# One core, 48 network steps in float32 halves: new orders on VectorE and ScalarE, and all the sums of a step's inner units on VectorE

## The chip, the core and the metric

One core of one Trainium2 chip runs the program. The metric is the device time of one execution, in microseconds (us). Engines: TensorE (PE, with its weight loads, PEld), VectorE (DVE), ScalarE (ACT), GpSimd (POOL), and SyncE (SP), which here only issues DMAs.

## The reference

`x` is (2, 2048, 512) in float32. Per batch entry b, three two-layer networks of 512 to 2048 to 512 units run over all tokens: an expert chosen by `itok_B_0_2[b]` and two shared ones. Their outputs are weighted by a softmax gate that is computed from the first token, and added to x; then one 512x512 matrix per entry, with a bias, is added.

```
s0, s1 = relu(x @ swi[0]) @ swo[0], relu(x @ swi[1]) @ swo[1]
eo     = relu(x @ wi[e]) @ wo[e]
w      = softmax(relu(concat(eo, s0, s1)[:, token 0] @ g1) @ g2)
x      = x + eo*w[0] + s0*w[1] + s1*w[2]
out    = x + (x @ W[c] + bias[c])
```

## The kernel before

**Tiling.** The 4096 tokens are four supers of 1024. A super takes 12 steps: three networks by four slices of 512 inner units, 48 steps in all. Step N consists of two up halves (n = 2N and 2N+1, 256 inner units each) and one down part. Each is a 2x2 block product by Strassen's scheme in Winograd's form, 7 products instead of 8. Each float32 operand is split into a high part (fp32r, copied by ScalarE: XH, WU, WD, HH) and a low part (original minus high, on VectorE: XL, WU, WD, HL), and a product is high x high + high x low + low x high. So an up product is 6 matmuls of 128x512 and a down product 12, and a step is 14*6 + 7*12 = 168 matmuls. Some steps carry 24 more, for the category matrix (`category`).

**The order of a step.** Every engine's order is written out by hand in a loop over m = -1 to 47. In step m the down part is that of step d = m and the up halves are a = 2N and b = 2N+1 of step N = m+1. TensorE's order is seven slots of up, up, down: a.0 a.1 and product 6 of the down part of step m-1; a.2 a.3 down.0; a.4 a.5 down.1; a.6 b.0 down.2; b.1 b.2 down.3; b.3 b.4 down.4; b.5 b.6 down.5. On the other engines `second(i)` stands for what follows a down product: VectorE adds its result to ACC (`add_sum`, L993 and L996), and where weights are being prepared, ScalarE (`down_high`, L710) and VectorE (`down_low`, L965) make the operands of a later down product.

**What an up half needs.** `first_product` (ACT L720), `seventh_product` (L726) and `chain` (L732, which fills u; product 4 waits for it) copy partial results; `block_22` (DVE L1007) and `block_21` (DVE L1016) finish two of four blocks of inner units. Product 6 waits for block_22, product 1 of the next half for block_21; relus follow on ScalarE.

**The sums.** From the four blocks of inner units, `hidden_sum` (L588) makes four sums for each half of the tokens' columns, eight a step, of 128x512. Before the change the four of half 0 run on GpSimd and the four of half 1 on VectorE. `hidden_high` (ACT L772) and `hidden_low` (DVE L976) split each operand of the down part; down product i waits for hidden_low i.

**The down part.** Product 1 is put on top of a copy of product 0, which ScalarE makes (`first_down_product`, L787) and which needs the banks of the step before to be free, so it waits for `add_sum(N - 1, 6)`.

**Preparing weights.** In the 12 steps of super 0 and in four of super 2, weights are met for the first time ("prepared"). GpSimd makes their block sums (`up_sums`, L604 to L609, and `down_sums`, L618 to L623), ScalarE and VectorE split them (`up_low`, L958), and SP stores the operands, which other supers load again. The GpSimd queue also makes the token sums of the next super (`token_sum`, L569, 128x1024), in steps 10, 22 and 34, whose tokens `token_high` (L682) and `token_low` (L949) split; up products of steps 11, 23 and 35 wait for them. `mix_add` (L1074) and what follows it weight the results of the super before, in some steps.

Queues run in the order of the program on each engine; waits are on semaphores. In VectorE's queue a step began, before the change, like this (a prepared step, token work left out):

```
for which in (0, 1, 3, 2): hidden_sum(dve, d, 1, which)
hidden_low 3, 1, 2;  add_sum(d - 1, 6) and one down_low
hidden_low 6;  up_low(b, 0);  one down_low;  block_22(a);  hidden_low 4
```

and ended `add_sum(d, 3)`, block_22(b), hidden_low(N, 0), `add_sum(d, 4)` and two down_low, block_21(b), up_low(b + 1, 1), `add_sum(d, 5)` and one down_low.

Of the kernel before, what the change touches and what calls it, by code (L numbers as in the profile page):

```python
# [57 lines left out]
LO_ORDER = [0, 3, 1, 2, 6, 4, 5]  # L58

# [110 lines left out]
def build(nc, xT, expert_id, category_id, wi, wo, swi, swo, g1, g2, W, bias, out):  # L170
# [11 lines left out]
    with ctx:  # L182
# [413 lines left out]
        def _(pool):  # L596
# [14 lines left out]
            def down_sums(N):  # L611
                k = 4 * PREP[N]
                A11, A12, A21, A22 = (PDR[:, q, :, :] for q in range(4))
                pool.wait_ge(s_pd, 16 * (PREP[N] + 1))
                if PREP[N] > 0:
                    pool.wait_ge(s_wld, PRODUCTS * PREP[N])

                pool.tensor_tensor(PDS[:, 0, :, :], A21, A22, ALU.add).then_inc(s_Sd, 1)  # L618
                pool.wait_ge(s_Sd, k + 1)
                pool.tensor_tensor(PDS[:, 1, :, :], PDS[:, 0, :, :], A11, ALU.subtract).then_inc(s_Sd, 1)  # L620
                pool.tensor_tensor(PDS[:, 2, :, :], A11, A21, ALU.subtract).then_inc(s_Sd, 1)
                pool.wait_ge(s_Sd, k + 2)
                pool.tensor_tensor(PDS[:, 3, :, :], A12, PDS[:, 1, :, :], ALU.subtract).then_inc(s_Sd, 1)  # L623
# [14 lines left out]
            for m in range(-1, STEPS):  # L638
# [3 lines left out]
                if d >= 0:  # L642
                    hidden_sum(pool, d, 0, 3)
# [7 lines left out]
                if N < STEPS:  # L651
                    hidden_sum(pool, N, 0, 0)
                    hidden_sum(pool, N, 0, 1)
                if end:
                    token_sum(pool, super_of(m) + 1, 2)
                if prepared(N):
                    down_sums(N)
                if N < STEPS:
                    hidden_sum(pool, N, 0, 2)
                if end:  # L660
                    token_sum(pool, super_of(m) + 1, 3)
                if m in (STEPS_SUPER, 3 * STEPS_SUPER):
                    category_identity(m // (2 * STEPS_SUPER))
# [9 lines left out]
        def _(act):  # L673
# [149 lines left out]
            for m in range(-1, STEPS):  # L823
# [10 lines left out]
                def second(i):  # L834

                    step, which = place_of(m, i)
                    if step >= 0:
                        begin_sum(step, which)
                    for e in made_after(step, which):
                        down_high(e // PRODUCTS, e % PRODUCTS)  # L840
# [5 lines left out]
                if more:  # L846
                    seventh_product(a)
                if m == -1:
# [8 lines left out]
                second(0)  # L857
                if d >= 0:
                    hidden_high(d, 6)
                if more:  # L860
                    chain(a)
                if start:
                    token_high(s + 1, 6)
                if more:
                    relu_11(a)
                if d > 0 and super_of(d) % 2 == 1 and rel == 1:
                    scale_sums(d)
                if d >= 0:
                    first_down_product(d)
# [73 lines left out]
        def _(dve):  # L943
# [161 lines left out]
            for m in range(-1, STEPS - 1):  # L1105
# [9 lines left out]
                def second(i):  # L1115
# [4 lines left out]
                    for e in made_after(step, which):  # L1120
                        down_low(e // PRODUCTS, e % PRODUCTS)
# [3 lines left out]
                    if m >= 0 and s % 2 == 0 and rel in (8, 9) and 1 <= i <= KD:  # L1125
                        gate_partial(s // 2, rel - 8, i - 1)

# [13 lines left out]
                if d >= 0:  # L1141
                    for which in (0, 1, 3, 2):
                        hidden_sum(dve, d, 1, which)
# [3 lines left out]
                if d >= 0:  # L1147
                    hidden_low(d, 3)
                    hidden_low(d, 1)
                    hidden_low(d, 2)  # L1150
                if start:
                    token_low(s + 1, 5)
                second(0)
# [34 lines left out]
                second(4)  # L1188
                out_part(1, 0)
# [9 lines left out]
                if gating:  # L1199
                    gate_max(s // 2)  # L1200
                block_21(b)
# [3 lines left out]
                if prepared_half(b + 1):  # L1205
                    up_low(b + 1, 1)
# [8 lines left out]
            for which in (0, 1, 3, 2):  # L1215
                hidden_sum(dve, t0, 1, which)
            for i in (3, 1, 2):
                hidden_low(t0, i)
            add_sum(t0 - 1, 6)
            hidden_low(t0, 6)  # L1220
            add_sum(t0, 1)
# [200 lines left out]
```

## Time and profile before

| | |
|---|---|
| median of 3 runs | 2019.12 us (2017.62 to 2020.86) |
| the profiled execution | 2017.75 us; its span on the core 2016.0 us |
| mean granted TensorE clock | 0.990 of full speed |
| busy share | PE 97%, DVE 65%, ACT 49%, POOL 27% |
| HBM | 223 GB/s over the span |

The 1.75 us between the profiled execution's time and its span lie around the program. All times in rows are counted from the span's start.

### The profile page before, as it was taken

The page shows a single profiled execution, that of the slowest core. Times are in us where ns is not written, and L with a number is a line of the kernel's source. Part 1 is how long each engine was busy: PE and PEld are TensorE (multiplying, and loading weights), DVE is VectorE, ACT ScalarE, POOL GpSimd, SP SyncE. Part 2 cuts the span into 40 slices and gives each one's busy share as a digit, 9 for nine tenths or more (in the row PEclk, how much of TensorE's full clock was granted, in tenths as well). Part 3 has the DMA queues.
Part 4 walks back from the last instruction along what each step waited for, and adds up shares of the span by engine and source line. Part 5 has one row for each costly group of instructions (what it writes and reads, how often), then busy time and mean ns, then how long its engine had stood idle before and what let it go on. Part 6 is the DMA issues. An engine that isn't in the chain of part 4 may idle for free. (4 is left out here: it accounts for less than half of the span.)

```text
span 2016.0 us, 25216 instructions
## 1 busy us (share of the span) xinstructions
PE 1950.9 (97%) x8504; PEld 1598.1 (79%) x8504; DVE 1317.7 (65%) x1378; ACT 981.4 (49%) x1441; POOL 542.3 (27%) x415
## 2 busy tenths in 40 slices
PE   6999999998999999999999999999989999999998
PEld 5777777786888888888788888887868788888886
DVE  6788788888645566455745554578885665555455
ACT  5655566556553444344544444456555533344441
POOL 4435534554112111111311111243541111111112
PEclk8999999999999999999999999999999999999999
DMA  5666656765876676566686676577658776756652
GB/s 214 237 246 258 256 224 250 303 259 221 260 246 215 203 234 215 181 196 195 226 267 200 198 225 203 190 280 271 263 199 264 242 231 208 219 184 194 196 168 107
DMA packets 187026, 450.99 MB, mean 224 GB/s; under 512 B 16916, under 2 KB 57876, under 8 KB 180500
## 3 DMA queue, kind: packets, MB, share of 16 engines
q1 hardware_dynamic: 186900, 449.39, 65.9%
q8 instruction: 70, 1.15, 0.2%
q14 instruction: 56, 0.46, 0.1%
HBM read 308.81 MB, written 140.51 MB: 223 GB/s over the span
## 5 line engine op out<-in xcount | busy, mean ns | idle before, releaser
L1268 PE MATMUL ups<-XH,WU 128*128 128x512 f32 x2688 | 895.1, 394 | 46.3 <-issue 24.2
L1268 PE MATMUL rps<-HH,WD 128*128 128x512 f32 x2688 | 884.8, 390 | 14.6 <-ACT rps L787 13.7
L1268 PEld LDWEIGHTS ups<-XH,WU 128*128 128x128 f32 x2688 | 508.7, 189 | 168.8 <-issue 26.1
L1268 PEld LDWEIGHTS rps<-HH,WD 128*128 128x128 f32 x2688 | 505.8, 188 | 125.7 <-ACT rps L787 18.7
L1268 PE MATMUL ups<-XL,WU 128*128 128x512 f32 x1344 | 526.9, 392 | 0.0
L1268 PE MATMUL rps<-HL,WD 128*128 128x512 f32 x1344 | 524.0, 390 | 0.0
L588 POOL TENSOR_TENSOR HT<-hid 128x512 f32<-128x512 f32 x96 | 136.8, 1424 | 944.1 <-PE rps L1268 944.1
L996 DVE SCALAR_TENSOR_TENSOR ACC<-rps,gw,ACC 128x1024 f32<-128x1024 f32 x129 | 165.3, 1282 | 221.4 <-PE rps L1268 221.2
L1268 PEld LDWEIGHTS ups<-XL,WU 128*128 128x128 f32 x1344 | 254.4, 189 | 51.3
L1268 PEld LDWEIGHTS rps<-HL,WD 128*128 128x128 f32 x1344 | 252.9, 188 | 52.1
L976 DVE TENSOR_TENSOR HL<-HT,HH 128x1024 fp32r<-128x1024 f32 x240 | 285.3, 1222 | 5.9 <-ACT HH L772 5.9
L772 ACT ACTIVATE HH<-HT 128x1024 fp32r<-128x1024 f32 x240 | 252.7, 1054 | 68.2 <-DVE HT L588 67.1
L993 DVE TENSOR_TENSOR ACC<-rps,ACC 128x1024 f32<-128x1024 f32 x124 | 151.3, 1220 | 105.9 <-PE rps L1268 105.8
L748 ACT ACTIVATE HT<-HT 128x512 f32<-128x512 f32 x96 | 60.7, 632 | 290.8 <-DVE HT L1016 290.7
L1007 DVE TENSOR_TENSOR hid<-ups,w 128x512 f32<-128x512 f32 x96 | 66.1, 688 | 131.4 <-PE ups L1268 131.4
L976 DVE TENSOR_TENSOR HL<-hid,HH 128x1024 fp32r<-128x1024 f32 x96 | 129.2, 1346 | 0.0
L740 ACT ACTIVATE hid<-ups 128x512 f32<-128x512 f32 x96 | 57.3, 597 | 128.4 <-PE ups L1268 128.4
L772 ACT ACTIVATE HH<-hid 128x1024 fp32r<-128x1024 f32 x96 | 101.7, 1059 | 23.4 <-PE rps L1268 21.8
L726 ACT ACTIVATE w<-ups 128x512 f32<-128x512 f32 x96 | 56.5, 589 | 112.3 <-PE ups L1268 112.3
L588 POOL TENSOR_TENSOR HT<-HT 128x512 f32<-128x512 f32 x48 | 64.7, 1347 | 137.1 <-PE rps L1268 137.1
L604 POOL TENSOR_TENSOR PUS<-PUR 128x256 f32<-128x256 f32 x32 | 24.8, 775 | 276.3 <-DVE WU L958 267.8
L744 ACT ACTIVATE hid<-hid 128x512 f32<-128x512 f32 x96 | 60.8, 633 | 72.9 <-DVE hid L1007 72.9
(105 smaller groups left out, 1607.9 us busy)
## 6 DMA issues: line engine op xcount, KB each, us to landing
WU<-wu_kept SPq DMA_DIRECT2D x448, 256.0 KB, 3.3
WD<-wd_kept SPq DMA_DIRECT2D x224, 512.0 KB, 3.3
wd_kept<-WD SPq DMA_DIRECT2D x112, 512.0 KB, 3.4
wu_kept<-WU SPq DMA_DIRECT2D x32, 1024.0 KB, 4.9
wu_kept<-WU SPq DMA_DIRECT2D x32, 768.0 KB, 3.7
sums_kept<-ACC SPq DMA_DIRECT2D x28, 512.0 KB, 5.2
MB<-sums_kept SPq DMA_DIRECT2D x28, 512.0 KB, 5.5
PUR<-in_L_cond_swi_dram SPq DMA_DIRECT2D x16, 512.0 KB, 6.1
```

What stands on the lines that cost most here:

```text
L588: eng.tensor_tensor(dst, p, q, op).then_inc(s_T[half], 1)
L604: pool.tensor_tensor(PUS[:, 2, :], A21, A22, ALU.add).then_inc(s_Su, 1)
L726: act.activation(w[:, :], ups[2][:, :], ACT.Copy).then_inc(s_w, 1)
L740: act.activation(hid[:, 0, half, :], ups[0][:, :], ACT.Relu).then_inc(s_relu, 1)
L744: act.activation(hid[:, 2, n % 2, :], hid[:, 2, n % 2, :], ACT.Relu).then_inc(s_relu, 1)
L748: act.activation(HT[:, 1, n % 2, :], HT[:, 1, n % 2, :], ACT.Relu).then_inc(s_relu, 1)
L772: act.activation(HH[:, i, :, :], src, ACT.Copy).then_inc(s_hhi, 1)
L976: dve.tensor_tensor(HL[:, i, :, :], src, HH[:, i, :, :].bitcast(F32), ALU.subtract).then_inc(s_hlo, 1)
L993: dve.tensor_tensor(ACC[:, j, :, :], src[:, :, :], ACC[:, j, :, :], ALU.add).then_inc(s_acc, 1)
L996: dve.scalar_tensor_tensor(out=ACC[:, j, :, :], in0=src[:, :, :], scalar=gw[:, g:g + 1], in1=ACC[:, j, :, :], op0=ALU.mult, op1=ALU.add).t ...
L1007: dve.tensor_tensor(hid[:, 2, half, :], ups[1][:, :], w[:, :], ALU.add).then_inc(s_ev, 1)
L1268: ins = pe.matmul(dst, stationary[a], moving[c], start=start and j == 0, stop=stop and j == 2, skip_group_check=True)
```

## The change

LO_ORDER, the order in which the low parts come, becomes 0, 1, 2, 3, 6, 4, 5. All eight sums of a step run on VectorE. On VectorE the step begins with three sums of half 1 and the last one of half 0, then the late `up_low`, and the `add_sum` of the step before stands behind one hidden_low instead of three; the down_low of the last slot is put off into the next step. The low parts of the next super's tokens (2 and 3) come ahead of the sums. On ScalarE `chain` is put ahead of hidden_high 6 and `first_down_product` ahead of `scale_sums`. GpSimd's `down_sums` is cut in two, with the last token sum between. The end of the program (from t0) gets the same order.

```diff
-LO_ORDER = [0, 3, 1, 2, 6, 4, 5]
+LO_ORDER = [0, 1, 2, 3, 6, 4, 5]
...
-            def down_sums(N):
+            def down_sums(N, late):
...
+                if late:
+                    pool.tensor_tensor(PDS[:, 2, :, :], A11, A21, ALU.subtract).then_inc(s_Sd, 1)
+                    pool.wait_ge(s_Sd, k + 2)
+                    pool.tensor_tensor(PDS[:, 3, :, :], A12, PDS[:, 1, :, :], ALU.subtract).then_inc(s_Sd, 1)
+                    return
...
@@ gpsimd, the loop @@
-                if d >= 0:
-                    hidden_sum(pool, d, 0, 3)
...
-                if N < STEPS:
-                    hidden_sum(pool, N, 0, 0)
-                    hidden_sum(pool, N, 0, 1)
                 if end:
                     token_sum(pool, super_of(m) + 1, 2)
                 if prepared(N):
-                    down_sums(N)
-                if N < STEPS:
-                    hidden_sum(pool, N, 0, 2)
+                    down_sums(N, False)
                 if end:
                     token_sum(pool, super_of(m) + 1, 3)
+                if prepared(N):
+                    down_sums(N, True)
@@ scalar @@
-                    for e in made_after(step, which):
+                    if i < PRODUCTS - 1:
+                        made(m, i)
+
+                def made(m, i):
+                    for e in made_after(*place_of(m, i)):
                         down_high(e // PRODUCTS, e % PRODUCTS)
...
                     seventh_product(a)
+                made(m - 1, PRODUCTS - 1)
...
                 second(0)
+                if more:
+                    chain(a)
                 if d >= 0:
                     hidden_high(d, 6)
-                if more:
-                    chain(a)
...
+                if d >= 0:
+                    first_down_product(d)
                 if d > 0 and super_of(d) % 2 == 1 and rel == 1:
                     scale_sums(d)
-                if d >= 0:
-                    first_down_product(d)
@@ vector @@
-                    for e in made_after(step, which):
-                        down_low(e // PRODUCTS, e % PRODUCTS)
+                    if 0 < i < PRODUCTS - 1:
+                        made(m, i)
...
-                if d >= 0:
-                    for which in (0, 1, 3, 2):
-                        hidden_sum(dve, d, 1, which)
                 if start:
                     token_low(s + 1, 2)
                     token_low(s + 1, 3)
                 if d >= 0:
-                    hidden_low(d, 3)
+                    hidden_sum(dve, d, 1, 0)
+                    hidden_sum(dve, d, 1, 1)
+                    hidden_sum(dve, d, 1, 3)
+                    hidden_sum(dve, d, 0, 3)
+                if m >= 0 and prepared_half(a):
+                    up_low(a, 1)
+                made(m - 1, PRODUCTS - 1)
+                if d >= 0:
                     hidden_low(d, 1)
-                    hidden_low(d, 2)
+                second(0)
                 if start:
                     token_low(s + 1, 5)
-                second(0)
+                if d >= 0:
+                    hidden_sum(dve, d, 1, 2)
+                    hidden_low(d, 2)
+                    hidden_low(d, 3)
+                made(m, 0)
...
                 second(4)
+                hidden_sum(dve, N, 0, 0)
+                hidden_sum(dve, N, 0, 1)
                 out_part(1, 0)
...
                     gate_max(s // 2)
+                hidden_sum(dve, N, 0, 2)
                 block_21(b)
...
-                if prepared_half(b + 1):
-                    up_low(b + 1, 1)
                 second(6)
@@ vector, the end @@
-            for which in (0, 1, 3, 2):
+            for which in (0, 1, 3):
                 hidden_sum(dve, t0, 1, which)
-            for i in (3, 1, 2):
-                hidden_low(t0, i)
+            hidden_sum(dve, t0, 0, 3)
             add_sum(t0 - 1, 6)
+            hidden_low(t0, 1)
+            hidden_sum(dve, t0, 1, 2)
+            hidden_low(t0, 2)
+            hidden_low(t0, 3)
+            add_sum(t0, 1)
             hidden_low(t0, 6)
-            add_sum(t0, 1)
```

## Rows read from the trace of the kernel before

**Rows 1.** The page: busy time of each engine, its share, instructions.

```profile
PE 1950.9 (97%) x8504; PEld 1598.1 (79%) x8504; DVE 1317.7 (65%) x1378; ACT 981.4 (49%) x1441; POOL 542.3 (27%) x415
```

**Rows 2.** Windows along step starts: stretch, its length, busy time (instructions), clock, DMA share, GB/s.

```profile
827.81:865.89 38.08, 38.08 (x170) 31.53 (x169) 20.82 (x21) 16.41 (x23) 5.21 (x4) 1.00 0.66 207
85.49:365.12 279.63, 270.77 (x1177) 219.42 (x1176) 227.24 (x248) 167.29 (x272) 132.60 (x113) 1.00 0.67 251
365.12:485.45 120.33, 116.31 (x505) 93.98 (x504) 100.86 (x112) 75.64 (x120) 57.39 (x44) 1.00 0.72 268
485.45:535.00 49.55, 40.85 (x169) 32.99 (x168) 35.81 (x33) 24.45 (x35) 16.05 (x10) 0.90 0.57 186
980.13:1020.42 40.29, 38.36 (x170) 31.45 (x168) 27.48 (x26) 20.02 (x28) 8.25 (x5) 1.00 0.61 196
1346.82:1466.77 119.95, 116.33 (x505) 93.97 (x504) 101.25 (x112) 74.98 (x119) 58.20 (x44) 1.00 0.71 267
1466.77:1515.53 48.76, 40.05 (x170) 32.43 (x169) 35.81 (x33) 24.26 (x35) 16.05 (x10) 0.93 0.58 191
```

**Rows 3.** Waits of TensorE in the whole span: us in total, times, longest.

```profile
PE ups L1268 <- issue: 24.2, 4, 8.1
PE rps L1268 <- ACT rps L787: 13.7, 12, 4.5
PE ups L1268 <- ACT u L732: 8.7, 11, 1.5
```

**Rows 4.** Timeline of VectorE in prepared step 3 (165.33 to 205.23): start, us.

```profile
167.68 0.69 DVE L958 TENSOR_TENSOR WU<-PUR,WU 128x512 fp32r<-128x512 f32 x1 [2.65 <-ACT WU L691]
...
171.03 1.22 DVE L588 TENSOR_TENSOR HT<-hid 128x512 f32<-128x512 f32 x1
...
174.72 3.49 DVE L976 TENSOR_TENSOR HL<-HT,HH 128x1024 fp32r<-128x1024 f32 x3
178.12 1.22 DVE L993 TENSOR_TENSOR ACC<-rps,ACC 128x1024 f32<-128x1024 f32 x1
...
182.61 0.68 DVE L1007 TENSOR_TENSOR hid<-ups,w 128x512 f32<-128x512 f32 x1
```

**Rows 5.** Timeline of TensorE in the same step.

```profile
180.58 0.50 PE L1268 MATMUL rps<-HH,WD 128*128 128x512 f32 x1 [0.69 <-ACT rps L787]
```

**Rows 6.** Timeline of GpSimd in the same step.

```profile
169.12 0.74 POOL L604 TENSOR_TENSOR PUS<-PUR 128x256 f32<-128x256 f32 x1 [2.24 <-DVE WU L958]
```

**Rows 7.** Groups of VectorE in the plain step of rows 2: busy, mean ns.

```profile
L588 DVE TENSOR_TENSOR HT<-hid 128x512 f32<-128x512 f32 x2 | 1.4, 688 | 0.0
```

**Rows 8.** The page's costliest groups, of the sums on GpSimd.

```profile
L588 POOL TENSOR_TENSOR HT<-hid 128x512 f32<-128x512 f32 x96 | 136.8, 1424 | 944.1 <-PE rps L1268 944.1
```

**Rows 9.** Timelines around the change of super, steps 10 and 11: VectorE, GpSimd, TensorE.

```profile
475.44 2.41 POOL L569 TENSOR_TENSOR XT<-XT,XS 128x1024 f32<-128x1024 f32 x1 [0.17 <-POOL XT L569]
...
480.11 0.68 DVE L1007 TENSOR_TENSOR hid<-ups,w 128x512 f32<-128x512 f32 x1
...
493.90 2.65 DVE L588 TENSOR_TENSOR HT<-HT,hid 128x512 f32<-128x512 f32 x1
...
493.21 2.79 POOL L569 TENSOR_TENSOR XT<-XT 128x1024 f32<-128x1024 f32 x1
...
500.06 0.76 PE L1268 MATMUL ups<-XH,WU 128*128 128x512 f32 x1 [8.08 <-issue]
```

**Rows 10.** Timeline of VectorE in mixing step 14.

```profile
649.86 1.60 DVE L1074 SCALAR_TENSOR_TENSOR MX<-MB,gw,MX 128x1024 f32<-128x1024 f32 x1 [5.81 <-DMA MX<-in_x_dram]
...
653.77 0.68 DVE L1007 TENSOR_TENSOR hid<-ups,w 128x512 f32<-128x512 f32 x1
```

**Rows 11.** Timeline of TensorE in step 13, where the sums are scaled.

```profile
590.13 0.50 PE L1268 MATMUL rps<-HH,WD 128*128 128x512 f32 x1 [1.38 <-ACT rps L787]
```

**Rows 12.** Timelines of VectorE and TensorE in the last step.

```profile
1968.24 1.28 DVE L996 SCALAR_TENSOR_TENSOR ACC<-rps,gw,ACC 128x1024 f32<-128x1024 f32 x1
...
1970.76 0.80 PE L1268 MATMUL rps<-HH,WD 128*128 128x512 f32 x1 [4.53 <-ACT rps L787]
```

More of the change, by code:

```diff
@@ L620, in down_sums @@
                 pool.tensor_tensor(PDS[:, 1, :, :], PDS[:, 0, :, :], A11, ALU.subtract).then_inc(s_Sd, 1)
-                pool.tensor_tensor(PDS[:, 2, :, :], A11, A21, ALU.subtract).then_inc(s_Sd, 1)
-                pool.wait_ge(s_Sd, k + 2)
-                pool.tensor_tensor(PDS[:, 3, :, :], A12, PDS[:, 1, :, :], ALU.subtract).then_inc(s_Sd, 1)
             def category_identity(b):
@@ L1126, in second, with made @@
                         gate_partial(s // 2, rel - 8, i - 1)
+                def made(m, i):
+                    for e in made_after(*place_of(m, i)):
+                        down_low(e // PRODUCTS, e % PRODUCTS)
                 def mix(half, net):
```

## The prediction, made before the result was known

> **What bounds the kernel now.** I read the busy times first: TensorE is busy for 97% of the span, VectorE for 65%, GpSimd for 27% [rows 1]. So what can be gained is TensorE's idle time and slow stretches, and nothing else. Then I cut the trace along the starts of the steps, by the first matmul of each up half a. A plain step (super 1, no weights prepared, nothing mixed) takes 38.08 us for 168 matmuls, 0.227 us each, with TensorE busy throughout: no order of the other engines makes it shorter. The reader is to compare the other windows with that: seven prepared steps (1 to 7) take 279.63, 39.95 each, 1.87 too long; steps 8 to 10 take 120.33 and 32 to 34 take 119.95, each 6 above 114.24; the first step of the second super takes 49.55, that of the fourth 48.76, that of the third 40.29 [rows 2]. The change can win there and at the end, and can lose in the rest.
>
> Third, TensorE's waits name who is late: ScalarE's copy of the first down product (L787) 13.7 us in 12 waits, its copy u (L732) 8.7 in 11, and 24.2 in 4 with no releaser named [rows 3]. The timelines say why. In prepared step 3 (start 165.33) the three hidden_low run 3.49 us from 174.72, and only then, at 178.12, comes the add_sum that L787 waits for; TensorE idles 0.69 before down product 1 [rows 4, 5]. VectorE's queue is late because it stood still for 2.65 us waiting for the late up_low at 167.68, and because its sums took up to 1.22 there, against 0.688 in a plain step [rows 4, 7]. At the change of super, up product 2 waits 8.08 for the low part of the tokens, which stands behind four sums, one of them 2.65 long [rows 9]. On VectorE and GpSimd, operations with two operands in SBUF stretch each other where they overlap.
>
> **The change part by part.** *The work moved.* 192 sums leave GpSimd (1.42 each [rows 8]) for VectorE at 0.69 [rows 7]: four a step, 2.8 us. VectorE is busy 20.8 of 38.1 in a plain step, 227.24/7 = 32.5 in a prepared one [rows 2]: 23.6, and at most 35.3, less what it no longer loses to GpSimd. It has room, so the question is only where it is late.
>
> *Prepared steps, the start.* From the step's first matmul (0) the new queue is: add_sum 1.2, four sums, two up_low, one down_low, one hidden_low, then add_sum. By durations 0.2 + 1.22 + 7*0.69 + 0.2 for two dependent sums + 1.22 gives 7.7 for its start; operations that don't wait start 0.08 before their predecessor's end (three of 1.22 took 3.49 [rows 4]), so about 7.1 to 8.3. Before it was 178.12 - 165.33 = 12.8 [rows 4]. ScalarE can then copy product 0 as soon as each half is made, by 11.7, and down product 1 wants it at 2.5 slots of 5.44, 13.6: that wait goes. The copy u stood behind hidden_high 2 and 6, hence behind the late sums; it now comes by 7.6 and is wanted at 10.9: gone too. Next in danger is block_22(a), wanted at 3 slots, 16.3; before, it ran at 182.61, 17.3 into the step. From add_sum: one sum, three hidden_low, two down_low, two up_low (0.42 and 0.69), 8 operations, about 6.2 start to start: start 14.4, end 15.1. That leaves 1.2, out of which GpSimd's four up_sums (0.74 each [rows 6], now starting at about 5.5 beside hidden_low 1, 2) may take all. I take back 1.6 of the 1.87: 7*1.6 = 11.2. For steps 8 to 10 and 32 to 34 the same two waits were 1.9, 1.45 and 1.0, and 1.5, 1.45 and 1.0: 8.3; the other 3.9 there lies with ScalarE's begin_sum and with the super's end, and stays.
>
> *The late up_low*, now after the sums, is done at 5.6 instead of 3.6. Behind it: up product 3 (wanted at 6.8), GpSimd's up_sums, and in SP's queue the store of the operands and the load of the next blocks, needed over 10 us later. Cost nothing, 1.2 us of cover. The four down_sums without hidden sums between them end earlier, and their readers are later: nothing.
>
> *Change of super.* Before, tokens 2 and 3 of the next super waited for the last token sum, which ran on GpSimd from 493.21 [rows 9], behind down_sums and a hidden sum. In the new order it comes before the second pair of down_sums and behind no hidden sums, so near 487, and token_low stands ahead of the four sums. The 8.08 wait goes, with it the matmuls at the lower clock right after (mean 0.90 in that step [rows 2]). But the two new sums before block_22(b) of step 10 now meet token sums: one ran 475.44 to 477.85, and in the new queue the next follows at once. block_22(b) ran at 480.11 and was wanted by 481.4 [rows 9]. Each of the sums and the token_low behind them can wait out a whole GpSimd operation (2.4, 2.4 and about 1.3): block_22(b) then ends near 484.6, 3.3 late. block_21(b) follows 1.5 late. And in step 11 VectorE still has everything before block_22(a): some 18 operations after 495, ready near 510.5, where TensorE would be at 507.6. The product then starts at 510.5 instead of 513.2: a gain of 2.7 a boundary if every lock falls badly, 7 if few do; I take 4.5, twice 9. The third boundary, step 23, loses 2.2 now [rows 2]; the same sums in step 22 may cost 1.5 of it: 0.5.
>
> A rule of the Trainium skill bears on this (SBUF — State Buffer, Who interferes with whom): a VectorE instruction with two SBUF inputs and a GpSimd instruction that reads SBUF exclude each other for the whole instruction. The trace agrees: 2.65 us for a 0.69 sum, beside a 2.79 token sum [rows 9].
>
> *Steps 13 and 37.* The four scalings (about 4.3) no longer stand ahead of L787: 1.38 of waiting [rows 11] and the slow matmuls after, 1.6 each: 3.2.
>
> *The end.* add_sum ran at 1968.24 and L787 came 4.53 late [rows 12]. With one sum and no hidden_low ahead it runs at 1964.9, and down product 1 then hangs on its hidden_low, ready at 1967.4: start 1967.5 instead of 1970.8, and less of it at the lower clock. A bound: nothing to 7 (the wait and the clock). GpSimd's first addition, now beside the sums, takes some back: 4.5.
>
> *What is lost.* Two sums (1.4) now stand between add_sum(d, 3) and block_22(b) in every step. In plain steps block_22(b) ends 3.2 us before it is wanted; in steps 14, 17, 38 and 41 VectorE has waited 5.81 for a load and block_22 (653.77) comes just in time or 0.4 late [rows 10]. There the sums fall on the path: 4*1.15 = 4.6, and 0.4 in the steps with about 1 us of slack. In step 0 the start of VectorE's queue meets GpSimd's down_sums with two sums more: 1.0.
>
> **Sum.** 11.2 + 8.3 + 9.0 + 0.5 + 3.2 + 4.5 - 5.0 - 1.0 = 30.7 us. The profiled execution, 2017.75, comes to 1987.0; it stood 1.37 under the median of 2019.12, so against that median 1988.
>
> **The rivals.** *Few locks fall badly:* the boundaries give 7 or more each, the mixing steps hide their sums behind other waits, step 0 costs nothing: 14 more, 1974. For it: the sums in plain steps are all 0.69. *The lock eats the boundaries:* each sum waits for a whole token sum, in steps 10, 22 and 34, and what was won at token_low is given back: 9.5 and 1.5 less, 1999. The 2.65 sum speaks for it [rows 9]; the earlier end of the token sums against. *The prepared steps trade waits:* L787 and u are in time, but block_22(a) is not, by 1 us in some 13 steps: 2001. It decides from 1.2 us of lost time between 5.5 and 14 us of the step. This and the one before are the Trainium skill's rule at work; both are priced here from rows. *VectorE becomes the bound (slower):* if the sums of half 0, now queued behind mixing and its loads, push block_22(b) past its 3.2 us of slack in the 32 steps without preparation. They must lose 4.3 us, not 1.4; each 1.1 beyond the slack costs 35 us in all: 2023. Against it: VectorE idles 17 of 38 there [rows 2]. *It doesn't do it:* the waits of L787 are ScalarE's own and stay: 2019; but L787 started 0.12 after add_sum's end, so no.
>
> **Numbers.** Chances: forecast 0.53 (its own range 1980 to 1996), few locks 0.13, boundaries eaten 0.14, waits traded 0.12, slower 0.04, no change 0.04. The range 1973 to 2005 takes in the first four and leaves out the last two and tails, 0.15. Faster by over 0.2% (4 us, about what a measurement can tell from no change) 0.92, within it 0.04, slower 0.04.
>
> **What would show it.** Windows: prepared steps near 38.3, plain steps 38.08 still, step 11 near 44, step 13 near 38.2. Waits: L787 under 4 us in all, u near nothing; block_22 (L1007) new, some 5 to 10. Groups: sums at 0.69 to 0.9 on VectorE, none on GpSimd; VectorE near 71% busy. I am wrong if the token sums of steps 10, 22 and 34 stretch and stay late, if ScalarE turns out late by its own queue, or if loads behind up_low come late.

## The result, and the profile after

The changed kernel takes 2005.24 us (median of 4 runs, 2004.06 to 2005.88) against 2019.15 for the kernel before on the same chip: ratio 0.993, interval 0.9913 to 0.9947. It is faster by 14 us where 31 were forecast, and 0.24 outside the forecast's range. The profiled execution took 2005.20 us, its span 2003.4. The profiled execution of the kernel before stood 1.4 under its median, so the spans differ by 12.6 and not by 14; the table below adds up to that.

The page's busy times answer to [rows 1]:

```profile
PE 1948.2 (97%) x8504; PEld 1597.6 (80%) x8504; DVE 1439.1 (72%) x1570; ACT 971.9 (49%) x1441; POOL 284.2 (14%) x223
```

192 instructions have gone from GpSimd to VectorE. Next the windows along the step starts of this trace, the answer to [rows 2]: a plain step, steps 1 to 7, 8 to 10, 11, mixing step 14, steps 32 to 34, step 35.

```profile
814.94:853.02 38.08, 38.08 (x170) 31.54 (x168) 23.39 (x25) 16.07 (x23) 0.00 (x0) 1.00 0.65 207
86.04:353.84 267.80, 267.80 (x1178) 220.13 (x1176) 244.29 (x276) 167.24 (x271) 101.90 (x84) 1.00 0.70 263
353.84:477.58 123.74, 116.45 (x505) 94.02 (x504) 114.77 (x123) 75.74 (x120) 49.57 (x35) 1.00 0.70 261
477.58:522.03 44.45, 40.29 (x169) 32.55 (x168) 35.48 (x39) 23.29 (x34) 2.98 (x2) 0.96 0.63 209
600.10:644.94 44.84, 43.81 (x194) 35.97 (x192) 26.89 (x29) 15.94 (x24) 0.00 (x0) 1.00 0.66 211
...
1334.81:1460.69 125.88, 117.92 (x506) 95.22 (x504) 116.75 (x125) 75.55 (x120) 50.31 (x36) 0.99 0.69 256
1460.69:1505.45 44.76, 41.02 (x170) 32.27 (x168) 33.83 (x38) 23.30 (x34) 1.41 (x1) 0.96 0.61 203
```

The table sets measured differences (after minus before, us) beside the forecast's terms. The forecast's 8.3 for steps 8 to 10 and 32 to 34 is split: 6.3 belong to steps 8, 9, 32 and 33, and 2.0 to steps 10 and 34.

| steps | measured | forecast |
|---|---|---|
| -1 and 0 | +0.5 | +1.0 |
| 1 to 7 | -11.8 | -11.2 |
| 8, 9, 32, 33 | +2.6 | -6.3 |
| 10, 11, 34, 35 | -2.3 | -11.0 |
| 22, 23 | +0.5 | -0.5 |
| 13, 37 | -3.4 | -3.2 |
| mixing steps | +3.8 | +5.0 |
| 46 to the end | -2.4 | -4.5 |
| sum | -12.6 | -30.7 |

Steps 11 and 35 alone did become shorter by 5.1 and 4.0; steps 10 and 34 became longer by 2.5 and 4.2 (39.35 to 41.89, 39.38 to 43.61). Two lines of the table hold the miss. TensorE's waits in the whole span, beside [rows 3], say to whom it now goes:

```profile
PE ups L1285 <- DVE hid L1008: 27.8, 22, 3.4
PE ups L1285 <- issue: 6.1, 1, 6.1
PE ups L1285 <- DVE HT L1017: 3.8, 2, 2.7
...
PE rps L1285 <- ACT rps L783: 1.3, 2, 1.1
...
PE ups L1285 <- ACT u L728: 0.4, 1, 0.4
```

What the change aimed at is gone: the copy of the first down product from 13.7 to 1.3, u from 8.7 to 0.4, the waits with no releaser from 24.2 in 4 to 6.1 in 1 (that one is in step -1 and was there before). In their place stands block_22 (L1008) with 27.8 in 22 waits, where 5 to 10 were forecast. Three timelines show it. First VectorE and GpSimd in prepared step 3 (start 162.47), beside [rows 4, 6]:

```profile
168.41 1.76 DVE L977 TENSOR_TENSOR HL<-HT,HH 128x1024 fp32r<-128x1024 f32 x1
170.10 1.21 DVE L994 TENSOR_TENSOR ACC<-rps,ACC 128x1024 f32<-128x1024 f32 x1
...
178.04 0.68 DVE L1008 TENSOR_TENSOR hid<-ups,w 128x512 f32<-128x512 f32 x1
...
169.05 1.73 POOL L604 TENSOR_TENSOR PUS<-PUR 128x256 f32<-128x256 f32 x1
```

add_sum starts 7.6 us into the step (forecast 7.7, before 12.8). block_22(a) starts at 15.57, where 14.4 was worked out from durations without contention: the 1.2 of slack went to GpSimd's up_sums, as the forecast feared (a hidden_low of 1.22 takes 1.76, an up_sum of 0.74 takes 1.73), and what is left just does. In step 8 (start 353.84) it doesn't:

```profile
383.39 1.78 DVE L959 TENSOR_TENSOR WU<-PUS,WU 128x512 fp32r<-128x512 f32 x1
385.09 1.78 DVE L1042 SCALAR_TENSOR_TENSOR gacc<-G,yv,gacc 128x512 f32<-128x512 f32 x1
386.80 1.78 DVE L587 TENSOR_TENSOR HT<-hid 128x512 f32<-128x512 f32 x1
388.68 1.59 DVE L587 TENSOR_TENSOR HT<-HT,hid 128x512 f32<-128x512 f32 x1
390.19 0.68 DVE L1008 TENSOR_TENSOR hid<-ups,w 128x512 f32<-128x512 f32 x1
...
386.29 1.74 POOL L615 TENSOR_TENSOR PDS<-PDR 128x512 f32<-128x512 f32 x1
...
371.34 0.50 PE L1285 MATMUL ups<-XH,WU 128*128 128x512 f32 x1 [1.02 <-DVE hid L1008]
...
390.93 0.50 PE L1285 MATMUL ups<-XH,WU 128*128 128x512 f32 x1 [0.68 <-DVE hid L1008]
```

Here four VectorE operations of about 0.7 each take 1.6 to 1.8, one behind another, while GpSimd's down_sums (1.3 where nothing meets them, as at 189.56) follow one another, one of them 1.74. Two of the four are the new sums, and one is a gate part (`gate_partial`, L1042), of which steps 8, 9, 32 and 33 have four each; the forecast never counted these. And step 10 (start 435.70), beside [rows 9]:

```profile
465.05 2.65 DVE L587 TENSOR_TENSOR HT<-hid 128x512 f32<-128x512 f32 x1
467.80 2.70 DVE L587 TENSOR_TENSOR HT<-HT,hid 128x512 f32<-128x512 f32 x1
470.43 2.28 DVE L950 TENSOR_TENSOR XL<-XT,XH 128x1024 fp32r<-128x1024 f32 x1
472.63 0.68 DVE L1008 TENSOR_TENSOR hid<-ups,w 128x512 f32<-128x512 f32 x1
...
475.98 3.46 DVE L966 TENSOR_TENSOR WD<-PDR,WD 128x512 fp32r<-128x512 f32 x2
479.36 1.75 DVE L587 TENSOR_TENSOR HT<-hid 128x512 f32<-128x512 f32 x1
...
464.75 2.40 POOL L568 TENSOR_TENSOR XT<-XT,XS 128x1024 f32<-128x1024 f32 x1 [0.17 <-POOL XT L568]
467.11 2.84 POOL L568 TENSOR_TENSOR XT<-XS 128x1024 f32<-128x1024 f32 x1
...
473.37 0.50 PE L1285 MATMUL ups<-XH,WU 128*128 128x512 f32 x1 [2.69 <-DVE hid L1008]
481.77 0.53 PE L1285 MATMUL ups<-XH,WU 128*128 128x512 f32 x1 [2.66 <-DVE HT L1017]
```

Each of the two sums lasts as long as a whole token sum beside it; block_22(b) is 2.69 late. The two down_low and the sum behind it are stretched too, by GpSimd's last token sum and down_sums, and block_21(b) is 2.66 late. The two down_low took 3.47 in the kernel before as well (at 483.48), where block_21(b) was only 0.63 late: new are the later start and the sum.

Steps 34 and 35 look alike but lost 0.2 where 10 and 11 gained 2.6. Most of the difference stands in the granted clock. Behind the wait of 2.83 us in step 34 it is at 0.50, the lower level of 1.2 GHz, for 3.4 us:

```profile
1454.91:1458.31 3.40, 3.40 (x8) 2.72 (x9) 3.40 (x3) 3.40 (x5) 3.40 (x2) 0.50 0.14 52
```

In step 10, behind its wait of 2.69, it stays at 1.00. Half of 3.4 is 1.7 us, and step 34 takes 1.72 more than step 10. Another 0.8 is that the kernel before was faster in steps 34 and 35 (88.13) than in 10 and 11 (88.90).

### The profile page after: what moved, and what is told of

Read it like the earlier page. It is cut to its first block and busy times, and to the rows that moved or that the text cites. A ratio compares the mean times of both kernels' runs of the same rounds, so it can differ in the third digit from the quotient of the medians.

```text
span 2003.4 us, 25216 instructions
## 1 busy us (share of the span) xinstructions
PE 1948.2 (97%) x8504; PEld 1597.6 (80%) x8504; DVE 1439.1 (72%) x1570; ACT 971.9 (49%) x1441; POOL 284.2 (14%) x223
## 5 line engine op out<-in xcount | busy, mean ns | idle before, releaser
L1285 PE MATMUL ups<-XH,WU 128*128 128x512 f32 x2688 | 898.4, 394 | 45.8 <-DVE hid L1008 27.8
L977 DVE TENSOR_TENSOR HL<-HT,HH 128x1024 fp32r<-128x1024 f32 x240 | 306.9, 1295 | 10.1 <-ACT HH L768 7.4
L587 DVE TENSOR_TENSOR HT<-hid 128x512 f32<-128x512 f32 x192 | 151.8, 791 | 7.5 <-PE rps L1285 5.2
L728 ACT ACTIVATE u<-ups 128x512 f32<-128x512 f32 x96 | 57.4, 598 | 111.5 <-PE ups L1285 111.5
L1008 DVE TENSOR_TENSOR hid<-ups,w 128x512 f32<-128x512 f32 x96 | 65.8, 685 | 46.4 <-PE ups L1285 45.5
```

The source lines that it names most:

```text
L587: eng.tensor_tensor(dst, p, q, op).then_inc(s_T[half], 1)
L728: act.activation(u[:, :], ups[1][:, :], ACT.Copy).then_inc(s_u, 1)
L977: dve.tensor_tensor(HL[:, i, :, :], src, HH[:, i, :, :].bitcast(F32), ALU.subtract).then_inc(s_hlo, 1)
L1008: dve.tensor_tensor(hid[:, 2, half, :], ups[1][:, :], w[:, :], ALU.add).then_inc(s_ev, 1)
L1285: ins = pe.matmul(dst, stationary[a], moving[c], start=start and j == 0, stop=stop and j == 2, skip_group_check=True)
```

## The experiments

**Theory.** The two halves of the change work against each other. The new orders are worth some 27 us. The move costs about 13 on top of them, because VectorE's sums read two operands in SBUF and wait out whole GpSimd operations (token sums, block sums) at places where block_22 has little slack. **Rivals:** the orders themselves bring less than forecast; the sums cost by VectorE's queue order alone, whatever GpSimd does; GpSimd is simply late.

### The orders alone, and the move alone

The changed kernel with the four sums of half 0 back in GpSimd's queue, at their old places, and gone from VectorE's:

```diff
@@ gpsimd @@
+                if d >= 0:
+                    hidden_sum(pool, d, 0, 3)
...
+                if N < STEPS:
+                    hidden_sum(pool, N, 0, 0)
+                    hidden_sum(pool, N, 0, 1)
                 if end:
                     token_sum(pool, super_of(m) + 1, 2)
                 if prepared(N):
                     down_sums(N, False)
+                if N < STEPS:
+                    hidden_sum(pool, N, 0, 2)
```

> The changed kernel with the four sums of half 0 back on GpSimd at their old places in its queue: the new orders without the move. Theory A (the orders win, the two moved sums ahead of block_22(b) lose): prepared steps 1 to 7 stay near 38.3 us, step 13 at 38.1, the waits for L1008-type block_22(b) in steps 14, 17, 22, 38, 41 fall back to what they were (0.5 a step), in all 1996 to 2001, faster than the changed kernel's 2005. Theory B (taking the sums from GpSimd is what frees VectorE from waiting at the shared port): prepared steps keep over 1 us of excess each and the time is 2008 or more.

(The second pair of down_sums stays behind the last token sum, as in the changed kernel.) And the kernel before with nothing but the move: those four taken from GpSimd, and on VectorE sum 3 behind the other four at the start of the step, sums 0 and 1 behind add_sum(d, 4), sum 2 ahead of block_21(b).

> The kernel before, with all eight sums on VectorE and none of the new orders: the fourth sum behind the four of half 1, two ahead of block_22(b), one ahead of block_21(b). Theory A: the prepared steps keep their 1.9 us and gain nothing, steps 14, 17, 38, 41 and the changes of super lose as in the changed kernel, in all 2022 to 2030. Theory B: prepared steps fall below 39.3 and the time is under 2015.

The orders alone take 1992.67 us (ratio 0.9867, 0.9851 to 0.9884), the move alone 2043.98 (1.012, 1.0103 to 1.0137), beside 2020.06 for the kernel before. The orders gain 27.4, the move alone loses 23.9, and together they gain 14: the move costs about 13 where the orders stand. Both times lie outside what was expected, the orders 3 us better than 1996 and the move 14 worse than 2030; half of its loss, 11.3 us, is in steps 8, 9, 32 and 33. Windows of the orders alone, steps 1 to 7, 8 to 10, 11, 14:

```profile
84.65:351.60 266.95, 266.95 (x1178) 220.43 (x1177) 228.68 (x248) 167.81 (x271) 137.75 (x113) 1.00 0.70 263
351.60:468.74 117.14, 115.47 (x506) 94.29 (x505) 102.84 (x112) 76.07 (x120) 61.18 (x44) 1.00 0.73 275
468.74:518.92 50.18, 42.90 (x169) 33.08 (x168) 34.73 (x33) 23.78 (x35) 16.66 (x10) 0.93 0.55 185
596.99:640.93 43.94, 43.80 (x193) 35.96 (x192) 25.48 (x25) 14.93 (x22) 5.79 (x4) 1.00 0.67 212
```

Steps 8 to 10 take 117.14 instead of 123.74, and step 14 is back at 43.94. But step 11 takes 50.18 against 44.45: with a sum on GpSimd between the token sums the tokens come late again. So the move has one use, at the change of super (5.7 and 4.0 us in steps 11 and 35), and costs 15.2 in steps 8 to 10 and 32 to 34, 3.9 in the mixing steps and about 4 in the rest (steps -1 and 0 1.4, 1 to 7 0.85, 22 and 23 1.1, the end 0.7). Windows of the move alone, steps 1 to 7 and 8 to 10, show the other side:

```profile
86.47:365.91 279.44, 269.84 (x1178) 219.59 (x1176) 241.87 (x276) 166.67 (x271) 95.19 (x84) 1.00 0.67 252
365.91:496.13 130.22, 118.92 (x506) 94.95 (x504) 113.99 (x124) 75.85 (x120) 46.44 (x35) 0.99 0.67 248
```

Without the orders the move leaves steps 1 to 7 where they were (279.63 before) and puts 9.9 on steps 8 to 10: what it does there, it does under either order.

### Where the sums stand on VectorE

The changed kernel with sums 0 and 1 of half 0 behind block_22(b):

```diff
                 second(4)
-                hidden_sum(dve, N, 0, 0)
-                hidden_sum(dve, N, 0, 1)
...
                 block_22(b)
+                hidden_sum(dve, N, 0, 0)
+                hidden_sum(dve, N, 0, 1)
```

> The changed kernel with the sums 0 and 1 of half 0 behind block_22(b) instead of ahead of it, nothing else. Theory A: the waits for block_22(b) go in the first step (3.4), in 8, 9, 32, 33 (about 1 each), 10 and 34 (2.7 and more), 14, 17, 22, 25, 38, 41 (0.4 to 1), some 15 us in all, of which a few come back at block_21(b) of steps 10 and 34: 1989 to 1994. Rival (VectorE is simply out of time there, whatever the order): the same waits turn up at block_21(b) or down products, 2002 or more.

It takes 1997.16 us (0.9892, 0.9876 to 0.9909), 8 less than the changed kernel; that is between the 1989 to 1994 expected and the rival's 2002. Step 14 falls from 44.84 to 43.52, its full pace, below the 43.95 of before as well; step 10 from 41.89 to 40.10. Step 11 rises from 44.45 to 46.76. VectorE and TensorE at the end of step 10 tell why:

```profile
471.14 1.16 DVE L587 TENSOR_TENSOR HT<-hid 128x512 f32<-128x512 f32 x1
472.41 1.60 DVE L587 TENSOR_TENSOR HT<-HT,hid 128x512 f32<-128x512 f32 x1
473.93 3.41 DVE L977 TENSOR_TENSOR HL<-hid,HH 128x1024 fp32r<-128x1024 f32 x1
...
481.27 0.68 DVE L1017 TENSOR_TENSOR HT<-ups,u 128x512 f32<-128x512 f32 x1
...
482.01 0.80 PE L1285 MATMUL ups<-XH,WU 128*128 128x512 f32 x1 [4.96 <-DVE HT L1017]
```

The wait moved down the queue: block_22(b) is 0.34 late, but what follows is stretched in its turn (a hidden_low of 1.22 takes 3.41) and block_21(b) comes 4.96 late. Order inside VectorE's queue removes the loss where GpSimd is idle, and passes it on where it isn't.

### The gate parts

The same kernel with the gate parts of steps 8, 9, 32 and 33 two slots later:

```diff
-                    if m >= 0 and s % 2 == 0 and rel in (8, 9) and 1 <= i <= KD:
-                        gate_partial(s // 2, rel - 8, i - 1)
+                    if m >= 0 and s % 2 == 0 and rel in (8, 9) and 3 <= i < 3 + KD:
+                        gate_partial(s // 2, rel - 8, i - 3)
```

> The same as the run before, and the four gate_partial of steps 8, 9, 32 and 33 two slots later, so none stands ahead of block_22(a) or block_21(a). Theory A: the waits of up product 6 of half a in those steps (1.3, 1.3, 1.8, 1.2) shrink to about 0.2: 4 to 5 us under the run before, 1985 to 1989. Rival (ScalarE's begin_sum holds them): less than 1.5 us.

1996.17 us (0.9883, 0.9866 to 0.9899) against 1997.16, and the two sets of runs overlap: not told apart in the total. In the steps it shows: step 8 goes from 41.43 to 40.33 and step 32 from 40.89 to 39.85; steps 9 and 33 move by 0.2. The gate parts hold block_22(a) up by about 1 us in each of steps 8 and 32, so they are a part of what was overlooked, and not the larger one. The total of 1996.17 is what the rival (under 1.5 us) had named, not the 1985 to 1989 expected: of the 2.5 us won in the four steps, step 23 lost 1.5 again (39.44 to 40.97) in the profiled executions.

### Does GpSimd count by what it reads?

In the changed kernel the token sums of the three later supers become a memset of their tile; in a second kernel the block sums (`up_sums`, `down_sums`) do. These sums are left out of the result.

```diff
-            eng.tensor_tensor(dst, p, q, op).then_inc(s_xT, 1)
+            if s > 0:
+                eng.memset(dst, 0.5).then_inc(s_xT, 1)
+                return
+            eng.tensor_tensor(dst, p, q, op).then_inc(s_xT, 1)
```

> The changed kernel, where the token sums of supers 1 to 3 are a memset of the same tile (the sums of the tokens are left out): GpSimd still writes the tile in the same place of its queue, but reads nothing. Theory A (the two moved sums of steps 10, 22 and 34 wait out whole token sums): the two sums of 2.65 and 2.70 us and the token_low of 2.28 fall to 0.7, 0.7 and 1.2 or near it, and the wait of 2.7 us for block_22(b) in step 10 and its like in 34 fall under 0.5. Rival (VectorE is late there by its own load): the wait stays over 1.5 us.

> The changed kernel, where the up_sums and down_sums of the weights are memsets (the block sums are left out): GpSimd reads nothing in the prepared steps. Theory A (block_22(a) is at the edge in steps 1 to 7 and late in 8 to 10 and 32 to 34 because GpSimd's reads hold VectorE up by 1.2 us in each step): block_22(a) of step 3 starts near 14.4 us into the step instead of 15.6, and the waits for block_22 in steps 8, 9, 32 and 33 fall under 0.3 each; steps 8 to 10 take under 119 us together instead of 123.7. Rival (the gate's parts and the moved sums alone fill VectorE): steps 8 to 10 stay over 121.5.

Without the reads of the token sums one run took 1989.39 us (step 10 38.91, step 34 38.91), without those of the block sums 1976.46 (steps 8 to 10 115.6 together, steps 1 to 7 38.08 each). But one memset is also shorter than the sum that it stands for (0.96 against 2.4 for tokens), so GpSimd was done sooner as well. The last two runs take that away: each token sum becomes three chained memsets, each block sum two.

```diff
+        def fill(eng, parts, last):
+            for n, dst in enumerate(parts):
+                ins = eng.memset(dst, 0.5)
+                if n < len(parts) - 1:
+                    ins.then_inc(s_pad, 1)
+                    pads[0] += 1
+                    eng.wait_ge(s_pad, pads[0])
+            ins.then_inc(last, 1)
...
+                fill(eng, (dst, dst, dst[:, :256]), s_xT)
...
+                fill(pool, (PUS[:, 0, :], PUS[:, 0, :]), s_Su)
```

> The changed kernel, with each token sum of the three later groups of tokens replaced by three memsets that follow one another on the same tile (two full ones and a half one, about 2.4 us by the 0.96 us of a full one in the run with unread tokens), so that GpSimd is busy about as long as with a token sum of 2.4 to 3.0 us and at the same places, but reads nothing. The token sums are left out of the result. Theory (a GpSimd instruction that reads SBUF and a VectorE sum of two SBUF inputs wait for each other): steps 10 and 34 take about 38.9 us each as in the run with the short memsets, the hidden sums beside them about 0.7 us, the total 1987 to 1992 us. Rival (what counts is how long GpSimd is occupied, so that its later work comes late): step 10 stays at 40.5 us or more and the total at 1995 us or more.

> The changed kernel, with each of GpSimd's block sums (up_sums, down_sums) replaced by two memsets that follow one another on its tile, so that GpSimd is occupied twice as long as in the run where one memset stood for each, and still reads nothing. The block sums are left out of the result. Theory (exclusion by reads): steps 8 to 10 take 115 to 118 us together (before 120.33, changed 123.75), the plain steps 38.08 us, block_22(a) of step 3 starts about 14.4 us into its step, the total is 1976 to 1981 us. Rival (GpSimd's occupation or its late results hold VectorE back): steps 8 to 10 take 121 us or more and the total is 1990 us or more.

With the tokens' memsets one run took 1992.04 us; step 10 38.90 and step 34 38.92. VectorE and GpSimd in step 10 (start 435.76), to be set beside the changed kernel's rows above:

```profile
465.12 0.68 DVE L603 TENSOR_TENSOR HT<-hid 128x512 f32<-128x512 f32 x1
465.91 0.69 DVE L603 TENSOR_TENSOR HT<-HT,hid 128x512 f32<-128x512 f32 x1
...
462.33 7.10 POOL L555 MEMSET XT<- 128x1024 f32 x9 [16.32 <-DMA XS<-in_x_dram]
...
473.87 2.35 POOL L555 MEMSET XT<- 128x1024 f32 x3 [0.77 <-issue]
```

The same sums start at the same time (465.12, 465.05) beside a GpSimd that is busy from 462.3 to 469.4 (before the edit 462.2 to 469.9), and take 0.68 instead of 2.65. The first theory holds, and the rival of a late GpSimd falls for step 10: it is the reading. In step 11 it is another matter: 40.46 us with the short memsets, 43.53 with the long ones, 44.45 in the changed kernel. There the time at which GpSimd finishes counts, 3.1 of the 4.0; in step 35 (40.72, 42.02 and 44.76) it is 1.3 of 4.0.

With the block sums' memsets one run took 1977.31 us. Windows of steps 1 to 7 and 8 to 10, and block_22(a) of step 3 (start 155.14):

```profile
78.98:345.54 266.56, 266.56 (x1177) 220.72 (x1176) 215.52 (x276) 170.21 (x272) 61.89 (x168) 1.00 0.70 263
345.54:461.18 115.64, 114.84 (x505) 94.46 (x504) 98.87 (x123) 75.70 (x118) 33.01 (x66) 1.00 0.74 276
```

```profile
169.51 0.68 DVE L1021 TENSOR_TENSOR hid<-ups,w 128x512 f32<-128x512 f32 x1
```

block_22(a) comes 14.37 us into the step, where the forecast worked out 14.4 for a VectorE that GpSimd doesn't hold. The memsets of step 3 last 2.68 us in all against 3.0 for four undisturbed sums of 0.74, and those of a step's down_sums 4.39 against 5.2 for four of 1.3, so GpSimd's occupation isn't fully restored; but doubling it moved the total by 0.85 us and steps 8 to 10 by 0.01. By this single run the block sums' reads cost the changed kernel some 28 us: 7.1 in steps -1 and 0, 1.2 in steps 1 to 7, 11.2 in steps 8, 9, 32 and 33, and 9.3 in 10, 11, 34 and 35, less 0.9 in the rest. The kernel before and the orders alone have these reads too; it is not the cost of the move, which is 13.

The Trainium skill (SBUF — State Buffer, Who interferes with whom) says that a GpSimd instruction that only writes doesn't exclude VectorE, while one that reads SBUF and a VectorE instruction with two SBUF inputs do exclude each other. These two runs agree: 0.68 beside a memset, 2.65 beside a token sum. The add_sum of step 3 above, with one operand in PSUM, takes 1.21 with GpSimd busy beside it. The memsets leave out the arithmetic of the sums as well as the reading; no run here tells these two apart.

### ScalarE's new places alone

The kernel before with `chain(a)` ahead of `hidden_high(d, 6)` and `first_down_product(d)` ahead of `scale_sums(d)`, and nothing else.

> The kernel before with ScalarE's two new places alone: chain ahead of hidden_high 6, first_down_product ahead of scale_sums. Steps 13 and 37 fall from 39.8 to 38.1 in either theory. Theory A (in prepared steps ScalarE is late because it waits for VectorE's sums): steps 1 to 7 gain at most 0.5 us each, 2012 to 2017. Rival (ScalarE's own order made the copies late): 1.0 or more each, under 2008.

2013.14 us (9 runs), 0.9967 (0.9957 to 0.9977). Step 13 falls from 39.78 to 38.09, steps 1 and 5 by 1.0 each, other prepared steps stay near 39.9. In them TensorE's waits for the copy of the first down product grow, from 13.7 to 16.6 over the span, as those for u shrink from 8.7 to 1.6: some 6 of the orders' 27 us are ScalarE's alone, and the other 21 need the rest of the new orders. Of these, VectorE's and the split of GpSimd's down_sums were not tried apart.

### A better version

The orders alone lost 5.7 us in step 11 to late tokens. So the last token sum goes ahead of sum 2 in GpSimd's queue:

```diff
+                if end:
+                    token_sum(pool, super_of(m) + 1, 3)
                 if N < STEPS:
                     hidden_sum(pool, N, 0, 2)
-                if end:
-                    token_sum(pool, super_of(m) + 1, 3)
```

> The new orders with the sums of half 0 on GpSimd, and there the last token sum ahead of hidden sum 2 instead of behind it. Theory A: token_low 2 and 3 of steps 11 and 35 come some 2 us sooner, so the wait at up product 2 (3.5 and 4.3 us with the slow matmuls after it) falls to 1 to 2 us: 1987 to 1990. Rival (the locks only fall elsewhere): 1992 or more.

1990.17 us (0.9854, 0.9838 to 0.9871), against 1992.67 (0.9867, 0.9851 to 0.9884) in another set of runs: the intervals overlap. Step 11 takes 47.58 instead of 50.18, step 35 49.17 instead of 48.73. Then the gate parts later as well:

> The run with the token sum sooner, and the four gate_partial of steps 8, 9, 32 and 33 two slots later. With the sums of half 0 on GpSimd, block_22(a) of these steps is late by 0.7, 0.8, 1.3 and 0.8 us, which is about what the gate's parts ahead of it take (0.5 to 0.75 each and a copy of 0.16). If they are what is left there: 2 to 3 us less, 1987 to 1988.5. Rival (the locks decide it, the gate's parts only fill time): under 1 us less.

1991.09 us (0.9855, 0.9838 to 0.9871): no gain where 2 to 3 us were expected. Step 8 fell from 39.67 to 38.65 and step 32 from 40.38 to 38.99, but steps 10 and 34 rose from 38.55 and 38.56 to 40.03 each. VectorE at the end of step 9 in this kernel (step 10 starts at 429.73) shows where it went:

```profile
429.01 1.77 DVE L1049 SCALAR_TENSOR_TENSOR gacc<-G,yv,gacc 128x512 f32<-128x512 f32 x1
...
432.44 0.74 DVE L1049 SCALAR_TENSOR_TENSOR gacc<-G,yv,gacc 128x512 f32<-128x512 f32 x1
433.10 0.68 DVE L587 TENSOR_TENSOR HT<-hid 128x512 f32<-128x512 f32 x1
```

The last two gate parts of step 9 now end 1.0 and 3.4 us into step 10, its sums begin at 433.10 instead of 431.11 (the kernel without this edit, step 10 at 429.77), and TensorE waits 1.18 for block_22(a). The other half of the idea, last, is to leave the sums of half 0 with GpSimd only in the steps near block and token sums, and to give them to VectorE behind block_22(b) elsewhere (the gate parts stay later):

```diff
+def sums_on_pool(N):
+    return N <= 13 or 22 <= N <= 24 or 31 <= N <= 37
```

> The run before, with the sums of half 0 on VectorE (0 and 1 behind block_22(b)) in the 23 steps that have neither prepared weights nor a change of super beside them, and on GpSimd in the others. If GpSimd's reads are the cost, the move is harmless there and takes GpSimd out of steps 14, 17, 38 and 41: these go from 43.95 to 43.52, 1.7 us less in all, every plain step stays at 38.08: 1985 to 1987. Rival (VectorE's queue is the cost anywhere): these steps grow and the time is 1989 or more.

1990.07 us (0.985, 0.9834 to 0.9866). Steps 14, 17 and 38 fall to 43.52, 43.71 and 43.55 from 43.95, as they should, and step 41 to 43.87 only. That is 1 us in all, less than these runs tell apart, and the total misses the 1985 to 1987 expected. Both versions near 1990 beat the kernel before by 29 us and the changed one by 15; of the two, the one with all sums of half 0 on GpSimd is simpler.

## Why the prediction was off

**Right.** The four main mechanisms. In steps 1 to 7 both waits went and block_22(a) was next at the edge (11.8 gained, 11.2 forecast). Steps 13 and 37 gained 3.4 (3.2). The wait for the tokens, 8.08, went: step 11 takes 44.45, "near 44" in the forecast. The two sums fell on the path of the mixing steps, for 3.8 (5.0); with the two sums behind block_22(b) step 14 went below its time of before, which shows the place. Steps -1 and 0 cost 0.5 (1.0). VectorE as the bound fell: plain steps still take 38.08.

**The first failed step** is "For steps 8 to 10 and 32 to 34 the same two waits were [...]: 8.3; the other 3.9 there [...] stays". The waits did go, but these steps differ from 1 to 7, and the text took them for the same. They have gate parts in VectorE's queue, and their down_sums meet the two new sums ahead of block_22(b), with no slack left there. The forecast applied the trade of waits ("waits traded", 0.12) to 13 steps at once, from a slack of 1.2; in fact it decided by step: 1 to 7 kept the gain, and steps 8, 9, 32 and 33 gave up 8.9. The orders alone show the size of the move's part here: steps 8, 9, 32 and 33 take 6.8 less with the four sums on GpSimd (157.37 against 164.13). The other 2.1 are about what the gate parts take: with the last token sum sooner, putting them later brought these steps from 157.99 to 155.58, and the forecast's 6.3 would have made 155.25. With the block sums unread steps 8 and 9 are at 38.4 and 38.1. The term's sources were loose too. The trace has the two waits in these six steps as 6.2 us; 8.3 takes some 0.3 more for each of the eight waits, which the forecast doesn't say. The windows leave 3.5 beside it, not 3.9 (120.33 + 119.95 - 228.48 - 8.3). And not all of that was ScalarE's: with the gate parts later and the sums on GpSimd, step 8 is at 38.65.

**The second** is the boundary, "I take 4.5, twice 9". Its lower end, a gain of 2.7 "if every lock falls badly", is what steps 10 and 11 gave: 2.6, with two sums of 2.65 and 2.70 and a token_low of 2.28 (2.4, 2.4 and about 1.3 priced). The text took a middle value although nothing in the queues kept the locks apart. block_21(b) was forecast 1.5 late and came 2.66 late, behind two down_low of 3.46 together (3.47 before) and a sum of 1.75; and steps 34 and 35 were taken for copies of 10 and 11, but lost 0.2 where those gained 2.6. The four gained 2.3 instead of 11.0: the rival "the lock eats the boundaries" happened, at nearly its price (9.5, measured 8.7). That its price was met so nearly is in part luck, for it named steps 10, 22 and 34 and not the lower clock in step 34. The chance of 0.14 was too low, since the row of 2.65 [rows 9] spoke for it and the sums stood right behind the token sums in time. In steps 22 and 23 the same made a gain of 0.5 a loss of 0.5.

**The third** is smaller: the end gave 2.4 instead of 4.5. Timelines of VectorE, GpSimd and TensorE there, beside [rows 12]:

```profile
1963.26 3.42 DVE L977 TENSOR_TENSOR HL<-HT,HH 128x1024 fp32r<-128x1024 f32 x1
...
1959.48 6.11 POOL L665 TENSOR_TENSOR XT<-XT,ACC 128x1024 f32<-128x1024 f32 x2 [429.18 <-DMA XT<-in_x_dram]
...
1967.93 0.50 PE L1285 MATMUL rps<-HH,WD 128*128 128x512 f32 x1 [2.25 <-DVE ACC L997]
```

The wait of 4.53 went down to 1.11, but a hidden_low of 1.22 took 3.42 beside GpSimd's additions, and TensorE waited 2.25 further on. The orders alone end only 0.7 sooner, so this has little to do with the sums.

In sum two rivals held at once, one nearly whole and one for four steps of 13, and the forecast had weighed them as if one excluded the other. 1988 + 8.9 + 8.7 is 2005.6. Steps 22 and 23 came out 1.0 worse than forecast and the end 2.1 worse, and the remaining terms 2.5 better, so that the nearness of this sum to 2005.24 is partly luck.

**Open.** Why the granted clock falls in step 34 and not in step 10, behind waits of nearly the same length, stays open. Steps -1 and 0 came near their forecast by a trade that it hadn't seen: in step -1 the two new sums take 1.76 and 1.63 beside down_sums and block_22(b) comes 3.40 late, but the two down_low behind them then take 1.28 instead of 3.44, and a wait of 2.58 for block_21(b) is gone. The runs with memsets are single ones, and their effect (13 and 28 us) is far above what one run can be off (the changed kernel's four lie within 1.8).

## What to carry to other kernels

Moving work to an engine with idle time is not priced by its duration there. Look at what the other engine still does at that moment: as long as GpSimd kept one stream of reads here, a VectorE instruction with both operands in SBUF lasted up to one GpSimd instruction longer (0.69 became 2.65 beside 2.40), so the moved work cost most in exactly the steps where GpSimd was busy. Put what TensorE waits for ahead of the moved work, and try the new order and the move apart, since one can hide what the other costs. And before one step's gain is multiplied by the number of steps, list what each of them has besides in its queues.

## What the runs showed of the hardware

- A VectorE sum of 0.69 us lasted 1.6 to 1.8 beside a row of GpSimd down_sums, and 2.65 to 2.70 beside token sums of 2.4 to 2.8; GpSimd's down_sums rose from 1.3 to 1.7 and token sums from 2.4 to 2.84 and 3.39. Beside memsets of the same length VectorE's sum stayed at 0.68.
- Taking 192 of GpSimd's 415 instructions away did not lessen the contention where it mattered: in steps 8 to 10 VectorE's busy time rose from 100.86 to 114.77, by 13.9 for 11 more instructions, which take 7.6 at 0.69 (against the orders alone, 102.84, by 11.9). TensorE's waits for block_22 fall from 22 (27.8 us) to 8 (6.4 us) with the four sums on GpSimd, and to 10 (11.5 us) with long memsets for block sums.
- A wait of TensorE can cost more than its length. In step 11 of the orders alone the waits are 0.60, 3.09, 0.21, 1.32, 0.30 and 1.77, together 7.3, but the step takes 12.1 more than a plain one. The granted clock is at 0.50 (1.2 GHz, not 2.4) from 479.40 to 482.79, right after the wait of 3.09, and from 496.47 to 499.86, after the one of 1.77. Of these 6.8 us TensorE waits 0.2; half of the rest, 3.3, is my estimate of what the clock costs, and 1.5 is not explained. In step 11 of the kernel before the clock is at 0.50 from 494.49 to 504.71, but for 5.6 of these 10.2 us TensorE was still in its wait of 8.08, so that the mean of 0.90 overstates the loss.
